# Routing the first image's tokens inside the second image's convolution

## What is computed

```python
x = x + conv_block(layernorm_over_channels(x))
t = tokens(x)                       # 2 x 9216 tokens of 256
t = t + moe(layernorm(t))
# conv_block: for dilation d in (1, 4, 8, 12):
f = softmax(conv3x3(x, w_d, dilation=d), over the 9 taps)
out_d = sum over the 9 taps of shifted x * f
y = conv1x1(concat(x, out_1, out_4, out_8, out_12), w_proj) + b_proj
return relu(group_norm(y, 32 groups of one image))
# moe: the top 2 of 8 experts for each token
out = tokens + sum over chosen e of weight_e * (gelu(tokens @ w1[e] + b1[e]) @ w2[e] + b2[e])
```

## Time and profile before

| | us |
|---|---|
| median of 3 runs | 2629.41 (2621.84 to 2630.81) |
| the profiled execution, its time | 2616.45 |
| its span from first to last instruction | 2614.6 |
| PE busy | 2046.2 (78%) |
| PEld busy | 1918.8 (73%) |
| DVE busy | 1624.7 (62%) |
| ACT busy | 1187.8 (45%) |
| POOL busy | 1026.5 (39%) |

### The profile page before, as it was taken

How to read it: one execution, slowest core, us unless ns; L and a number is a source line. 1 busy time by engine, 2 the same in 40 slices (tenths; PEclk the granted TensorE clock), 3 DMA queues, 4 the chain that set the end, 5 groups by cost and what they waited for, 6 DMA issues and landing times.

```text
span 2614.6 us, 61081 instructions
## 1 busy us (share of the span) xinstructions
PE 2046.2 (78%) x20292; PEld 1918.8 (73%) x20293; DVE 1624.7 (62%) x4238; ACT 1187.8 (45%) x2441; POOL 1026.5 (39%) x1390
## 2 busy tenths in 40 slices
PE   5887699999688867999994766750799999995332
PEld 4777499999678757999993766650799999994222
DVE  3554475666555545656665867663577899885644
ACT  4654233333256533333333544440577777773211
POOL 4444012233234411223320677777455566563000
PEclk9999599999899977999996655555899999997555
DMA  4332156677433214656766897753566555555887
GB/s 122 91 88 68 47 174 157 158 179 176 123 85 85 79 43 132 170 142 170 174 160 186 277 325 264 257 189 131 164 195 206 172 162 159 150 158 177 289 296 271
DMA packets 328031, 434.91 MB, mean 166 GB/s; under 512 B 86586, under 2 KB 253114, under 8 KB 326778
## 3 DMA queue, kind: packets, MB, share of 16 engines
q1 hardware_dynamic: 273618, 315.07, 42.9%
q0 software_dynamic: 41024, 97.10, 10.7%
q10 hardware_dynamic: 13200, 20.19, 2.1%
HBM read 278.46 MB, written 159.94 MB: 168 GB/s over the span
## 4 chain that ended last, share of the span: by engine, by line
PE 46%; DMA 17%; POOL 15%; issue 10%; DVE 5%; ACT 4%; DVEq 2%; SPq 1%; POOLq 0%; ACTq 0%
PE ps_y L381 16%; POOL expert_in L1786 8%; DMA expert_out<-e_out,dest 7%; PE ps L381 6%; POOL taps L1752 6%; PE ps_o L854 6%; PE ps_a L381 5%; PE ps_b L790 5%; DMA o_y<-expert_out 3%; DMA o_acc<-res_scratch 2%; ACT g_rows L1059 2%; PE ps_f L762 2%; DMA expert_in<-c_ln,pos 2%; PE ps_o L841 1%; PE ps_x L967 1%
## 5 line engine op out<-in xcount | busy, mean ns | idle before, releaser
L381 PE MATMUL ps_y<-cat_hi,wp 128*128 128x288 f32 x2048 | 469.5, 305 | 1.8 <-DVE cat_lo L1370 1.8
L1774 POOL DMA_DIRECT2D patches<-rows_scratch x352 | 194.8, 598 | 651.5 <-PE ps_o L854 492.4
L1809 POOL DMA_INDIRECT expert_out<-e_out,dest x304 | 310.3, 1021 | 237.4 <-DMA expert_out<-e_out,dest 117.4
L1786 POOL DMA_INDIRECT expert_in<-c_ln,pos x288 | 294.4, 1022 | 186.8 <-DVE pos L1515 92.1
L381 PEld LDWEIGHTS ps_y<-cat_hi,wp 128*128 128x128 f32 x2048 | 343.2, 189 | 2.0 <-DVE cat_lo L1370 2.0
L1137 ACT ACTIVATE cat_hi<-ps_o 128x288 fp32r<-128x288 f32 (+1 forms) x576 | 200.1, 386 | 252.9 <-PE ps_o L854 164.2
L381 PE MATMUL ps_y<-cat_lo,wp 128*128 128x288 f32 x1024 | 301.4, 294 | 0.0
L1370 DVE SCALAR_TENSOR_TENSOR cat_lo<-ps_o,cat_hi 128x288 fp32r<-128x288 f32 (+1 forms) x576 | 219.4, 419 | 129.8 <-ACT cat_hi L1137 129.6
L1752 POOL TENSOR_TENSOR taps<-taps,g_rows 96x108 f32<-96x108 f32 (+1 forms) x432 | 200.7, 494 | 242.2 <-ACT g_rows L1059 238.5
L381 PE MATMUL ps<-e_hi,w_now 128*128 128x256 f32 x1216 | 243.8, 284 | 1.2 <-issue 1.1
L381 PE MATMUL ps<-w,h_hi 128*128 x1216 | 234.5, 291 | 5.6 <-DVE h_lo L1658 5.6
(11 more groups left out here) (181 smaller groups left out, 4774.1 us busy)
## 6 DMA issues: line engine op xcount, KB each, us to landing
e_x<-expert_in SPq DMA_DIRECT2D x152, 260.0 KB
o_y<-expert_out SPq DMA_DIRECT2D x48, 768.0 KB, 5.3
patches<-rows_scratch SPq DMA_DIRECT2D x160, 192.0 KB
patches<-rows_scratch SPq DMA_DIRECT2D x256, 108.0 KB
patches<-rows_scratch SPq DMA_DIRECT2D x192, 112.0 KB
x_in<-in_x SPq DMA_DIRECT2D x48, 384.0 KB, 3.3
rows_scratch<-rows_st SPq DMA_DIRECT2D x48, 384.0 KB, 3.1
y_scratch<-y_acc SPq DMA_DIRECT2D x16, 1152.0 KB, 11.6
```

The source lines that it names most:

```text
L381: mm = eng.matmul(out, lhs[p], rhs[q], start=start and n == 0, stop=stop and n == 2)
L1774: pool.dma_start(patch_target(s, n), patch_source(m, s, n)).then_inc(patch_pooled[s % RING], 16)
L1786: pool.indirect_dma_start(out=xs_dram, out_offset=bass.IndirectOffsetOnAxis(ap=at, axis=0), in_=c_ln[:, v, k // TT, k % TT], in_offset=Non ...
L1809: pool.indirect_dma_start(out=ys_dram, out_offset=bass.IndirectOffsetOnAxis(ap=at, axis=0), in_=e_out[:, u, j], in_offset=None).then_inc(e ...
```

## The change

1. The routing of the first image moves into the second image's convolution. From step 2 on, one `slot` a step (two in kind 3, 78 in all) is put behind a unit of `branch`. In a slot TensorE transposes one tile of 128 tokens and multiplies it by the router weights, before the norm, into a bank `ps_k`; the norm is applied afterwards to the 8 logits (`router_sum`, `r_rstd`, `r_nmr`). ScalarE copies the tile out of PSUM at the next unit (`keep_slot`), so that the bank is free for the next slot, and later makes the residual and the normalised rows from that copy. VectorE's moments, choice and placement are cut into parts of a few instructions, one part a unit. GpSimd scatters a pair in three parts of 4.
2. `ps_b` becomes one bank to make room for `ps_k`. Band, relu and remainder of a step are done in two halves, the second behind unit 1.
3. `RING` is 3 instead of 4, for both images, to make room in SBUF. `EARLY` is 28 instead of 30.
4. In the second image GpSimd begins only every third of the 18 loads of kind 3; SP begins all others, and also the loads of x and y blocks (256 tokens) and the residual stores of the first image. ScalarE begins the first two blocks.
5. The routing stage does the 12 pairs of the second image. Its constants are loaded at the kernel's start; expert weights, biases and filler rows come right behind the loads of its first two pairs. The group norm's factors of the first image are computed at the start of the second image's taps stage.

The diff, cut to its core (the remaining parts are declarations, the split of `wp` into two tiles, the same factors written as functions, and counts with CPAIRS in place of PAIRS):

```diff
-RING = 4
+RING = 3
...
 KEPT = 6
 TILES = TOKENS // 128
+ITILES = PIX // 128
+HELD = 3
+BT = 2
+BLOCKS = ITILES // BT
...
-EARLY = 30
+EARLY = 28
...
-            ps_b = psum(r1, "ps_b", [128, 2, 512])
+            ps_b = psum(r1, "ps_b", [128, 512])
+            ps_k = psum(r1, "ps_k", [128, 512])
...
+        slot_ticks = []
+        for s_ in range(2, STEPS):
+            first = 2 if kind(s_) == 1 and s_ > UNITS1 else 1
+            slot_ticks += [unit(s_) + first] + ([unit(s_) + 5] if kind(s_) == 3 else [])
+        slots = {u: k for k, u in enumerate(slot_ticks)}
+        pair_ends = {slot_ticks[TP * p + TP - 1]: p for p in range(CPAIRS)}
+        pair_ranks = {slot_ticks[TP * p + RANK_AT]: p for p in range(CPAIRS)}
+        step_of_tick = [s_ for s_ in range(STEPS) for n_ in range(CC * parts(s_))]
+
...
+        def second_queue(m, s, n):
+
+            if m:
+                return n % 3 == 2 and kind(s) == 3
             return n % 2 == 1 if kind(s) == 3 else kind(s) == 0 and n >= 6
...
+            for dst, src in ((same[:], a["k_same"]), (router[:], a["router"]), (order[:], a["k_order"]),
+                             (before[:], a["k_before"]), (region[:], a["k_region"]), (token[:], a["k_token"])):
+                sp.dma_start(dst, src).then_inc(consts_in, 16)
...
+                        if not second_queue(m, s, n):
                             sp.dma_start(patch_target(s, n), patch_source(m, s, n)).then_inc(patch_loaded[s % RING], 16)
...
+                def load_block(j):
+
+                    after(sp, r_tok, BT * (j - RX + 1))
+                    sp.wait_ge(r_x1, j - RY + 1)
+                    here = slice(j * BT * 128, (j + 1) * BT * 128)
+                    sp.dma_start(r_x[:, j % RX], x_dram[0, :, :, here]).then_inc(r_loaded[j % RX], 16)
+                    sp.dma_start(r_y[:, j % RY], y_dram[0, :, :, here]).then_inc(r_loaded[j % RX], 16)
+
+                def store_residual(g):
+
+                    sp.wait_ge(r_resd, TT * (g + 1))
+                    half = g % 2 * TT
+                    sp.dma_start(res_dram[g], r_res[:, half:half + TT].rearrange("p k c -> p (k c)")).then_inc(r_stored[g % 2], 16)
+
...
+                blocks, kept = RY, 0
                 for s in range(STEPS):
+                    while m and blocks < BLOCKS and slot_step(max(0, BT * (blocks - RX) + 1)) + 3 <= s:
+                        load_block(blocks)
+                        blocks += 1
+                    while m and kept < 2 * CPAIRS and residual_step(kept) + 3 <= s:
+                        store_residual(kept)
+                        kept += 1
                     load_patches(s)
                     behind = s - UNITS1 - 18
                     if behind >= 0 and behind % 12 == 0:
                         store_rows_of(behind // 12)
...
+                while m and kept < 2 * CPAIRS:
+                    store_residual(kept)
+                    kept += 1
...
+            load(1, 1)
+            sp.dma_start(etiles[:], a["k_etiles"]).then_inc(consts_in, 16)
+            sp.dma_start(w_stage[:].rearrange("p e c -> p (e c)"), a["w1"]).then_inc(w_loaded, 16)
+            sp.dma_start(b1[:], a["b1"]).then_inc(b_loaded, 16)
+            sp.dma_start(b2[:].rearrange("p e c -> p (e c)"), a["b2"].partition_broadcast(128)).then_inc(b_loaded, 16)
+            for e in range(E):
+                sp.dma_start(xs_dram[E * CAP + e * S:E * CAP + (e + 1) * S], a["k_fill"][E + e]).then_inc(zeroed, 16)
+            with sp.Fori(1, CPAIRS // 2) as t:
+                for v in range(2):
+                    load(t * 2 + v, v)
+                    store(t * 2 + (v - 2))
...
+                    j, k = divmod(t, BT)
+                    pe.wait_ge(r_x1, j + 1)
+                    for c in range(CC):
+                        pe.transpose(ps_k[:, c * 128:(c + 1) * 128], r_x[:, j % RX, c, k * 128:(k + 1) * 128], ident[:])
+                    for c in range(CC):
+                        mm = pe.matmul(ps_k[:, 256 + t % TP * E:256 + (t % TP + 1) * E], r_x[:, j % RX, c, k * 128:(k + 1) * 128],
+                                       router[:, c], start=c == 0, stop=c == CC - 1)
+                    mm.then_inc(r_tok, 1)
+
+                def rank_pair(p):
...
+                    pe.matmul(out, before[:, 0], r_either[:].rearrange("p t e -> p (t e)"),
+                              start=True, stop=False, skip_group_check=True)
...
+                def slot(k):
+
+                    after(pe, r_kept, slots_before(k))
+                    if ranked_in(k) is not None:
+                        rank_pair(ranked_in(k))
+                    if k < ITILES:
+                        turn_tile(k)
...
                 for s in range(STEPS):
                     if s + 1 < STEPS:
-                        band(s + 1)
+                        band(s + 1, 0)
                     for n in range(CC * parts(s)):
                         branch(s, n // parts(s), n % parts(s))
+                        k = due(m, s, n, slots)
+                        if k is not None:
+                            slot(k)
                         if s and n in (1, 3):
                             project(s - 1, n // 2, 0)
                             project(s - 1, n // 2, 1)
+                        if n == 1 and s + 1 < STEPS:
+                            band(s + 1, 1)
...
+                    act.dma_start(r_x[:, j], x_dram[0, :, :, here]).then_inc(r_loaded[j], 16)
+                    act.dma_start(r_y[:, j], y_dram[0, :, :, here]).then_inc(r_loaded[j], 16)
...
+                    act.wait_ge(r_loaded[j % RX], 32 * (j // RX + 1))
+                    for c in range(CC):
+                        last = act.activation(r_y[:, j % RY, c], r_y[:, j % RY, c], ACT.Relu,
+                                              bias=gn_bias[:, 0, c:c + 1], scale=gn_scale[:, 0, c:c + 1])
+                    last.then_inc(r_relu, 1)
...
+                        act.wait_ge(r_tok, k + 1)
+                        if k % TP == 0 and p >= HELD:
+                            act.wait_ge(r_scattered[p % HELD], 16 * TP * TOP * (p // HELD))
+                        last = act.activation(r_ln[:, p % HELD, k % TP, 0:C], ps_k[:, 0:C], ACT.Copy)
...
+                            after(act, r_read, p - 1)
+                            last = act.activation(r_raw[:, p % 2], ps_k[:, 256:256 + TP * E], ACT.Copy)
...
+                        act.wait_ge(r_ranked, p + 1)
+                        after(act, r_based, p)
+                        last = act.activation(r_count[:], ps_k[:, 304:304 + (TP + 1) * E], ACT.Copy)
+                    if k < ITILES or p is not None:
+                        last.then_inc(r_kept, 1)
...
+                        after(act, r_stored[i // TT], 16 * p)
+                    act.activation(r_res[:, i], r_ln[:, p % HELD, i, 0:C], ACT.Identity,
+                                   bias=r_nmr[:, p % 2, i:i + 1], scale=r_more[:, p % 2, i:i + 1]).then_inc(r_resd, 1)
+
+                def norm_tile(p, i):
+
+                    act.activation(r_ln[:, p % HELD, i, 0:C], r_ln[:, p % HELD, i, 0:C], ACT.Identity,
+                                   bias=r_nmr[:, p % 2, i:i + 1], scale=r_rstd[:, p % 2, i:i + 1]).then_inc(r_lnd, 1)
+
...
+                            band_hi(s + 1, 1)
+                        if m and s == 0 and n == 3:
+                            relu_block(0)
+                        k = due(m, s, n, slots, 1)
+                        if k is not None:
...
+                        k = due(m, s, n, slots, 2)
+                        if k is not None and k % BT == 0 and k // BT + 1 < BLOCKS:
+                            relu_block(k // BT + 1)
...
+                            p = due(m, s, n, pair_ends, 6 + 2 * i)
+                            if p is not None:
+                                residual(p, i)
+                            p = due(m, s, n, pair_ends, 7 + 2 * i)
+                            if p is not None:
+                                norm_tile(p, i)
...
+                def band_hi(s, j):
+
+                    k, first, n = KIN[kind(s)], j * halves(s)[0], halves(s)[j]
+                    act.wait_ge(band_ready, 2 * (m * STEPS + s) + j + 1)
+                    act.activation(bands[0:k, s % 2, 0, first:first + n], ps_b[0:k, 0:n], ACT.Relu).then_inc(band_hi_done, 1)
...
+                    dve.tensor_tensor(r_x[:, j % RX], r_x[:, j % RX], r_y[:, j % RY], ALU.add).then_inc(r_x1, 1)
...
+                    dve.bn_stats(r_stats[:], r_ln[:, p % HELD, i, 0:C]).then_inc(r_stat, 1)
+                    dve.wait_ge(r_stat, t + 1)
+                    dve.bn_aggr(r_mv[:, p % 2, i], r_stats[:]).then_inc(r_moment, 1)
+
...
+                def pick_step(ins):
+
+                    ins.then_inc(r_picked, 1)
+                    picked[0] += 1
+                    dve.wait_ge(r_picked, picked[0])
...
+                        dve.tensor_tensor(r_pick[:, 0], raw, every(r_rstd[:, p % 2]), ALU.mult).then_inc(r_read, 1)
...
```

(42 more changed lines are left out.)

467 lines of the change are left out of this document (308 added, 159 removed).

## The result

The changed kernel takes 2609.40 us (median of 7 runs, 2600.39 to 2613.36), the kernel before 2623.17 (7 runs): ratio 0.9934, 95% interval 0.9909 to 0.9958. It is 13.8 us faster where 80 were forecast (2549, range 2490 to 2612): just inside the upper end of the range, with a sixth of the gain. The profiled execution took 2611.34 with a span of 2609.5, against 2616.45 and 2614.6. The 80.5 us that the sum promised shrank to 5.1 between these two executions.

A forecast was written before the change was run, and what follows sets the result against it. TensorE bounds the convolutions and GpSimd routing; after the change SP's issue time bounds the second convolution. Terms: -194.5 + 13 + 30 + 54 + 12 + 2 + 3 = -80.5 us, giving a median of 2549, range 2490 to 2612.

The forecast's parts named there:

- SP's time to begin loads: Second convolution: SP's issue time becomes the bound; first 16 steps +30 us, the 16 later cycles +54.
- SP, per cycle: 20.4: Second convolution, three-step cycle: SP's patch loads 15.7 us, y stores 1.9, block loads 1.7, residual stores 1.1; sum 20.4.
- Part 2: The forecast's section on extra work in the second convolution, engine by engine: +30 us in the first 16 steps, +54 in cycles.
- TensorE's slot: Second convolution: two transposes and two small products per tile take 0.41 us, making a TensorE cycle 19.5 us.
- rival 1: TensorE stays the convolutions' bound, SP's issuing hides; second convolution +39 us, first unchanged, whole kernel 2492; chance 0.17.
- Ring of three: First convolution: three ring places cost 4 us behind each of three y stores, +12; in the second, inside SP's sum.
- Routing: Last stage: 12 pairs instead of 24, GpSimd's scatters still the bound, half of 389.1 us goes: -194.5.
- Weights: Start of routing: expert weights, biases and filler rows behind the first two pairs' loads delay the first scatter, +13 us.
- tail: Between second convolution and routing: the last pair's 12 scatters end near the y store, +2 us.
- 2, VectorE: Second convolution: VectorE, given 148 us more, becomes the bound in kind 1 steps; +42 us, whole kernel 2591; chance 0.15.
- 3, landing: Both convolutions: patch landing decides with the three-deep ring; +251 us instead of 84, whole kernel 2716; chance 0.06.
- 4: Routing isn't hidden: the first image's scatters trail behind the convolution, at worst 183 us, whole kernel 2732; chance 0.03.

The follow-up runs named there:

- b_spq: Kernel before, ring of four, with the changed kernel's share of patch loads between SP and GpSimd in the second image; 2667.54 us, ratio 1.0164.
- a_oldq: Changed kernel with GpSimd beginning its old patch loads again in the second image; 2575.79 us, ratio 0.9816.
- a_wait3: As a_pool, but SP keeps the waits that stood ahead of the block loads; 2593.23 us, ratio 0.9882.
- a_pool: Changed kernel with GpSimd instead of SP beginning all block loads of the first image's routing, with their waits; 2572.99 us, ratio 0.9805.
- a_mix: Changed kernel: GpSimd begins block loads, its two old kind 0 loads and every third of kind 3; y stores in four parts; 2540.11 us, ratio 0.9683.
- b_ring3: Kernel before with three ring places instead of four in both images, nothing else; 2671.10 us, ratio 1.0191.
- a_best: Changed kernel with the edits of a_oldq and a_pool, y stores in four parts and each third of scatters paced by TensorE; 2570.49 us, ratio 0.9811.

## Why the prediction was wrong, step by step

- **What bounds the kernel, and SP's time to begin loads: right.** SP's beginnings from 1028 on sum to 442.5 us, some 452 with the 12 loads begun ahead of that, where 117 + 16 x 20.4 = 443 was said; b_spq and a_oldq show that the convolution follows them. The first 16 steps took 121.6 us against the 117 of the text. So the miss is in the cycles: +117 us where +54 was said, twelve of 23.4 us without a store, three of 32.6 with one, and 2.3 us in the last.
- **"SP, per cycle: 20.4", taken as the whole cycle: the step that failed.** It added up what SP begins and left out what SP waits for. Part 2 priced the block loads at 1.7 us a cycle and never named the wait in front of them, or the patches queued behind it. Measured: 44.1 us of such waits, and SP waits 3.1 us in each cycle without a store; a_wait3 against a_pool shows that not waiting is worth 20.4 us and not beginning 13.5. The 0.5 us that was added for other engines stood in its place. The other part is size: outside store cycles SP needs 19.0 + 1.3 us, not 18.5. What remains of the miss is in the next two points; no run parts their shares in the changed kernel.
- **TensorE's slot: mis-sized.** 0.61 us against 0.41, so a cycle is 20.4 us and not 19.5. That is as much as SP begins in a cycle without a store, so relieving SP gave 34 to 36 us and not 56 or 90, and with rival 1 as I priced it (413 us) the best kernel still takes 463. TensorE is busy 60 us more in a_mix than in the kernel before, where 36 to 40 were said.
- **Clock: left out.** The gaps brought the granted clock to 0.91; at 0.93 a cycle of work takes 21.99 us instead of 20.62. TensorE does the same products in 450 us here and in 431 in a_mix, at 0.96 to 0.98.
- **Ring of three: right place, too small.** About 6 us a store (b_ring3), 4 said, and 3 to 5 us in a cycle without a store, which was not foreseen; the first convolution +24.3 instead of +12. The upper end was 10.
- **Routing: right, in part by luck.** The scatters took 192.3 us less, and 194.5 was said. Weights +4.6 against +13 (below the upper bound that I took), tail +8.4 against +2: residual stores and scatters of the last pair end at 1561, behind the y store. These three sum to -179.3, and -179.5 was said, since the last two misses cancel.
- **Output: +7.8 against +3,** of 230 us; not pursued. Nor was the experts' -4.6.
- **Rivals.** 1, TensorE as the bound, was wrong for this kernel and nearly holds in a_mix, but not at its price. 2, VectorE: busy 345 of 519, 109 us more than before where 148 were summed (12.3 us a pair leaves 0.1 us for an aggregate, which no row gives); never the longest wait of TensorE (10.9 us for cat_lo, by the waits). 3, landing: not the bound, but not absent. b_ring3's cycles without a store are unchanged but for one, and in the changed kernel 14 us of TensorE's gaps are patches that landed late while the DMA engines were nearly full. 4: the last scatter of the first image starts 12 us behind the convolution. The slower side was reached after all, on the other chips, by a mechanism that no rival had.
- **The range** ended at rival 2, and that the time still lies in it, 3 us from its end, is no merit of the sum. A wait added to a queue that was called full already was worth a bound of its own: each of the 34 waits for a block between nothing and SP's longest wait of before, 3.9 us, would have reached well beyond 2612.

## What to carry to other kernels

When a queue is forecast to be full, add its new waits to its new work, and ask of each wait what stands behind it in the same queue; moving loads to an engine that has time (GpSimd, 188 of 519 us busy) gave 34 to 36 us of the second convolution; cutting the stores gave 3 to 7, hardly more than two executions differ. But a_best shows that such an engine fills up too. A prefetch ring must cover the longest single thing its queue does, not the mean: a 6.9 us store passed unseen with four places and cost about 6 us with three, and cut in four, on a queue with slack, nothing that can be seen. Work hidden inside another stage is paid there at that stage's price: the 192 us taken from routing cost 150 us in the convolution, and 95 in the best order found. And the gain of 0.7% on one chip was a loss of 0.8% on another.

## What the hardware showed unexpectedly

- On two chips bursts of 8 or 12 indirect DMAs of 128 rows mostly go with 7 to 15 us in which TensorE starts an instruction every 0.7 us or a multiple of it, and SP, in one such stretch, a DMA every 1.04 us; on the others no such stretch stands behind the same bursts. The kernel before differs by 107 us between them (2731 against 2624); where, no trace shows.
- A product of 8 columns costs almost what one of 128 does when its stationary side is new: four f32 passes in 0.36 us, 0.09 each, with weight loads of 201 ns, beside two transposes of 128 columns in 0.25 us.
- The DMA behind two strided stores of 1.15 MB can hold SP for 4.7 us, as a block load at 1290.74 did, though beginning one takes 0.4 us otherwise.
